# Attention block in exact-split fp32: value matmuls issued ahead of the score matmuls, and four engines' lists reordered

## The reference

```python
xn = layernorm(x, g_in)
q = (xn @ Wq).reshape(b, n, H, DH).transpose(0, 2, 1, 3) * scale
k, v = split(xn @ Wkv)                      # one head each, null_kv put in front
sim = einsum('bhid,bjd->bhij', q, k) + bias # null column, causal and padding masks
attn = softmax(sim, axis=-1)
out = einsum('bhij,bjd->bhid', attn, v)     # to b, n, H * DH
return x + layernorm(out @ Wo, g_out)
```

## Time and profile before

| what | value |
|---|---|
| median of three runs | 1016.31 us (1016.21 to 1018.83) |
| the profiled execution | 1017.48 us, span 1015.7 us |
| TensorE busy | 989.0 us (97%) |
| GpSimd busy | 834.8 us (82%) |
| VectorE busy | 767.9 us (76%) |
| ScalarE busy | 658.6 us (65%) |
| mean granted TensorE clock | 0.995 |

### The profile page before, as it was taken

The page is one execution under the profiler, slowest core; times in us unless marked ns, Lnnn a source line. Parts: engine busy times, 40 slices in busy tenths (PEclk is TensorE's granted clock), DMA queues, the critical chain, the costliest instruction groups (busy, mean ns, idle before and its releaser), DMA issues.

```text
span 1015.7 us, 43757 instructions
## 1 busy us (share of the span) xinstructions
PE 989.0 (97%) x14250; PEld 869.1 (86%) x14250; DVE 767.9 (76%) x3553; ACT 658.6 (65%) x2622; POOL 834.8 (82%) x1503
## 2 busy tenths in 40 slices
PE   7889999999999999999999999999999999999987
PEld 5879888888888888888888888888888888888875
DVE  5976787777887777787777887777787777786664
ACT  5846676665676665676665676666676666675563
POOL 4877888888888888888888888888888888888786
PEclk9998999999999999999999999999999999999999
DMA  8422223223232332323323232232323223222112
GB/s 240 118 79 73 86 72 87 82 68 98 64 107 73 80 87 60 105 69 87 79 70 96 68 106 72 76 90 55 109 70 86 78 71 96 68 70 67 37 44 63
DMA packets 93774, 84.04 MB, mean 83 GB/s; under 512 B 25328, under 2 KB 67824, under 8 KB 93552
## 3 DMA queue, kind: packets, MB, share of 16 engines
q1 hardware_dynamic: 92496, 81.05, 29.9%
q10 hardware_dynamic: 1056, 0.04, 0.1%
HBM read 40.12 MB, written 16.78 MB: 56 GB/s over the span
## 4 chain that ended last, share of the span: by engine, by line
PE 89%; POOL 4%; SPq 3%; issue 2%; DVE 1%; DMA 1%; ACT 1%; POOLq 0%; DVEq 0%; ACTq 0%
PE ps_proj L569 39%; PE ps_pv L546 22%; PE ps_pv L553 11%; PE ps_s L507 10%; PE ps_pv L532 8%; SPq L369 1%; POOL bias_b L1222 1%; POOL w_nrm L1231 1%; DMA q_sb<-in_fside_16xSxS_dram 0%; SPq L344 0%; SPq L379 0%; SPq L338 0%; POOL bias_c L1320 0%; POOL y_nrm L1271 0%; POOL y_out L1275 0%
## 5 line engine op out<-in xcount | busy, mean ns | idle before, releaser
L1031 ACT ACTIVATE exp_bot<-logit_bot,neg_max 128x129 f32<-128x129 f32 x512 | 201.4, 398 | 211.0 <-DVE neg_max L693 208.2
L1222 POOL TENSOR_TENSOR bias_b<-bias_c,mask_add 128x256 f32<-128x256 f32 (+1 forms) x512 | 297.9, 612 | 26.8 <-DVE neg_max L693 26.4
L569 PE MATMUL ps_proj<-xt_hi,wq_hi 128*128 128x256 f32 x1024 | 299.0, 292 | 6.0 <-ACT v_raw L1083 3.7
L569 PE MATMUL ps_proj<-xt_hi,wq_lo 128*128 128x256 f32 x1024 | 285.0, 278 | 0.0
L569 PE MATMUL ps_proj<-xt_lo,wq_hi 128*128 128x256 f32 x1024 | 284.6, 278 | 0.0
L693 DVE CUSTOM_DVE_ANT_0 logit_bot<-ps_s,bias_b 128x128 f32<-128x128 f32 x512 | 128.5, 289 | 139.7 <-PE ps_s L507 123.1
L569 PEld LDWEIGHTS ps_proj<-xt_hi,wq_hi 128*128 128x128 f32 x1024 | 193.4, 189 | 21.2 <-issue 10.5
L1231 POOL TENSOR_TENSOR w_nrm<-exp_bot,w_inv 128x256 f32<-128x256 f32 x256 | 157.9, 617 | 63.0 <-DVE w_inv L702 61.6
L546 PE MATMUL ps_pv<-wo_hi,o_hi 128*128 128x512 f32 x488 | 194.1, 398 | 1.5 <-DVE o_lo L715 1.4
L569 PEld LDWEIGHTS ps_proj<-xt_hi,wq_lo 128*128 128x128 f32 x1024 | 194.0, 189 | 0.7 <-issue 0.5
L569 PEld LDWEIGHTS ps_proj<-xt_lo,wq_hi 128*128 128x128 f32 x1024 | 193.6, 189 | 0.0
(11 more groups left out here) (114 smaller groups left out, 1747.3 us busy)
## 6 DMA issues: line engine op xcount, KB each, us to landing
x_in<-in_x_dram SPq DMA_DIRECT2D x32, 512.0 KB, 4.1
x_split<-xn SPq DMA_DIRECT2D x480, 32.0 KB, 1.9
v_rep<-v_raw SPq DMA_DIRECT2D x256, 32.0 KB, 1.9
x_res<-in_x_dram SPq DMA_DIRECT2D x128, 64.0 KB, 1.9
x_res<-in_x_dram SPq DMA_DIRECT2D x64, 128.0 KB, 2.6
out_dram<-y_out SPq DMA_DIRECT2D x128, 64.0 KB, 1.7
out_dram<-y_out SPq DMA_DIRECT2D x64, 128.0 KB, 2.3
w_raw<-in_L_cond_Wq_dram SPq DMA_DIRECT2D x4, 512.0 KB, 7.6
```

What stands on the lines that cost most here:

```text
L569: mm = pe.matmul(ps[:, 0:TOK], w[:, k, cols], xt[:, slot, k], start=(j == 0), stop=(j == len(todo) - 1))
L1031: ins = nc.scalar.activation(out_[:, s, j], in_[:, s, j], ACT.Exp, bias=neg_max[:, s, k:k + 1], scale=-1.0, accum_out=w_sum[:, s, k:k + 1])
L1222: ins = nc.gpsimd.tensor_tensor(out_, bias, key_mask, ALU.add)
```

## The change

Five lists are reordered, and one wait is added; what is computed stays the same. On TensorE, the `values` of a visit come ahead of the `scores` of the same step. On VectorE, the first of the four `heads_lo` of a visit comes ahead of the `logits` of that step, the other three stay where they were. On ScalarE, `heads_hi` comes ahead of both halves of the step's exponentials at every visit; before, at `t` = 6 and 14, the later half of the exponentials came ahead of it. On SyncE, in the first body (`p = 0`) the values of the second group are spread before the mask load and before `split_x(3)`. GpSimd waits for VectorE's three pieces of `wo_lo` before it makes the fourth.

```diff
@@ SyncE, body, p = 0
                     split_x(BY_PE)
                     next_x(0)
+                    spread_v(2 * p + 1)
                     next_mask()
                     split_x(2 * p + 3)
                     next_x(1)
-                    spread_v(2 * p + 1)
@@ TensorE, body
                 for t in steps(first, last):
+                    for batch, back in due("pv", p, t, first, last):
+                        values(p, batch, back)
                     if t % 2 == 0 and t < CP:
                         scores(p, t)
-                    for batch, back in due("pv", p, t, first, last):
-                        values(p, batch, back)
                     for f, slot, kind, i in front_parts(p, t, first, last):
                         front(f, slot, kind, i)
@@ VectorE, body
                         early = parts[:1] if not list(due("heads", p, t, first, last)) else []
+                        for batch, back in due("heads", p, t, first, last):
+                            heads_lo(batch, 0)
                         if t < CP:
                             logits(n, t)
...
                         for batch, back in due("heads", p, t, first, last):
-                            for g in range(4):
+                            for g in range(1, 4):
                                 heads_lo(batch, g)
@@ ScalarE, body
                     n = CP * p + t
-                    if t < CP and t % CG != STEP_HEADS:
-                        exponentials(n, t, 1)
                     for batch, back in due("heads", p, t, first, last):
                         for g in range(4):
                             heads_hi(batch, g)
-                    if t < CP and t % CG == STEP_HEADS:
+                    if t < CP:
                         exponentials(n, t, 1)
-                    if t < CP:
                         exponentials(n, t, 0)
@@ GpSimd, first_group
                 pool.wait_ge(wo_hi_made, WP)
+                pool.wait_ge(wo_lo_made, WP - 1)
                 nc.gpsimd.tensor_tensor(wo_piece(wo_lo, WP - 1), raw_piece(WP - 1, OT // WP),
```

## The result

The changed kernel takes 1036.14 us (median of 4 runs, 1034.39 to 1037.18), the kernel before, beside it, 1017.31 us (1016.21 to 1018.83): a ratio of 1.0183, 95% interval 1.0164 to 1.0202. It is slower by 1.8% where I forecast 1012.6 us, and above the range (to 1018.0). The profiled span grew from 1015.7 to 1032.6 us, by 16.9.

A forecast was written before the change was run, and what follows sets the result against it. TensorE was taken as the bound, busy throughout the steady loop. Terms -6.5 + 9.9 - 5.7 - 1.5 = -3.8 us gave 1013.7 profiled, forecast as 1012.6 us for the timed median; range 1008.0 to 1018.0.

The forecast's parts named there:

- Fetches: Projection matmuls behind the value matmuls at t = 2: breaks without a releaser would be hidden, -1.5 us (0 to -1.9).
- The start: First body: v_rep issued earlier removes TensorE's 3.67 us idle and the slow clock behind it, 6.5 us sooner (5.8 to 7.2).
- The wait of 0.8 without a fall of the clock: Start, before the third projection block: a wait of about 0.8 us is left, with no clock fall expected from it.
- V ahead of S at t = 2 and 10: Value matmuls before score matmuls wait for transposes or y_nrm: 0.34 us at 29 visits, +9.9 us (5.5 to 18.9).
- the restart: Value matmuls at t = 2 and 10 begin 0.14 us after the transposes they waited for, read from one visit.
- the 0.06 for GpSimd: At the value matmuls of t = 2 and 10, y_nrm late by some 0.06 us more in the mean.
- weight load was pulled across the wait: Alternative at the value matmuls' wait: weights loaded early, a visit costs 0.19, the whole some 4 us less; not expected.
- o_lo ahead of the logits at t = 6 and 14: Output matmuls no longer wait for the first o_lo: 0.20 us at 29 visits, 5.7 us won, low bound 2.8.
- GpSimd: not the bound: Rival: GpSimd's later w_nrm delays y_nrm and the value matmuls, 0.65 a visit, sum +5.2, 1021.5 us; chance 0.23.
- the three rivals: GpSimd becomes the bound (1021.5 us, 0.23); value matmuls hardly wait (1008.1, 0.17); the start doesn't pay (1018.0, 0.1).

The follow-up runs named there:

- late o_lo in the old order: Kernel before with SyncE's and GpSimd's edits only, plus the last three o_lo at t = 14 moved behind a copy and two transposes on VectorE: 1028.14 us.
- early o_lo in the new order: Changed kernel with all four o_lo ahead of the logits at t = 6 and 14: 1030.04 us, 1.0153.
- all four written-out kernels: TensorE's loop unrolled in the changed kernel (1016.41 us), the start alone (1010.38), S first at t = 2 (1013.61) and the best kernel (1001.95).
- S first at t = 2: Changed kernel with scores ahead of values again at t = 2 and 10, values still first at t = 6 and 14: 1029.58 us, 1.0148.
- the start alone: Kernel before with only SyncE's and GpSimd's edits, visits still scores then values: 1012.00 us, 0.9974.
- the second profile: The unchanged kernel before, profiled again for its start: 1013.85 us, span 1012.0.
- the best kernel: The start alone with TensorE written out, ScalarE's list as changed, first o_lo between the two steps' logits at t = 6 and 14: 1001.95 us, 0.9870.
- its two looped forms: The best kernel with TensorE's loop kept: 1012.13 us; then also with all four o_lo ahead of the second logits at t = 14 alone: 1007.97 us.
- S first everywhere: Changed kernel with TensorE's order alone undone, scores ahead of values at every visit, loop kept: 1030.38 us, 1.0143.

## Why the prediction was wrong, step by step

**The step that failed is "Fetches", -1.5 us, between 0 and -1.9.** I saw breaks of 0.1 to 0.4 without a releaser in the F behind V, took them for something that a TensorE standing at V would have hidden, and did not ask what they were. They are the array running out of instructions, and with those ahead of S at t = 0, for which my sum had no term, they grew by 17 us. Break (a): O to S went from 5.87 to 6.41; taken over the 5.59, and without the 0.11 of O's slow first matmul in the old figure, 0.17 became 0.82: 13 x 0.65 = 8.5. Break (b): F to O went from 1.59 to 2.27, 13 x 0.68 = 8.9. With +17.4 in place of -1.5 my sum is -6.5 + 9.9 - 5.7 + 17.4 = +15.1; the spans differ by 16.9.

The cause of (a) is shown, from both sides: late o_lo in the old order bring it (+16, of which 2 are the array's own wait), early o_lo in the new order take it away, and without the jump there is none of it, with the last o_lo anywhere from 1.16 to 2.73 after O's start: S then starts 0.32 after the start of O's last matmul in all four written-out kernels, against 1.54 in S first at t = 2 with its loop. By the Trainium skill (Runtime: NRT & Kernel Launch, section "Instruction fetch mechanics") a sequencer fetches the next page of instructions while it executes the current one, in a purely sequential way, and a taken branch to a page outside the window must wait for that page. The runs agree: 16 KB a packet, 9 packets a pair with the jump and 7 without, and breaks of this kind only with the jump. That crossing a page is otherwise "mostly hidden", as that section of the Trainium skill says, holds for the written-out kernels (between 85 and 940 us no break of over 0.15 us that is not a wait for data) and not for (b).

For (b) the runs show less. At its full size it needs V ahead of S at t = 2 and the loop: F to O is 1.52 with S first at t = 2 and 1.49 to 1.50 written out, against 2.27. It is not always gone with S first: the other loops of that order have 1.59 to 1.76. In the kernel before, the fetch next to this visit started 0.29 us before V (mean of 13), in the changed one 1.29 after V's start. How much of that shift comes from V's wait and how much from S now standing behind V was not separated.

**The start: right in size for the execution I read, in part by luck, and too large for others.** The wait of ScalarE for v_rep is gone, the clock's row is at 9 throughout, SyncE issued x_split(3) from 56.90 (I had it start as before, at 56.08; in the start alone it is 58.16), the third F waited 0.82 us (about 0.8 forecast), and V of step 14 is where I put it (77.4):

```profile
74.41 0.38 PE L569 MATMUL ps_proj<-xt_hi,wq_hi 128*128 128x256 f32 x1 [0.82 <-DVE q_sb L777]
...
77.33 1.43 PE L532 MATMUL ps_pv<-wt,v 32*64 32x128 f32 x80
```

But 87.68 belongs to that one execution. Measured against the second profile, 82.98, the changed start's 81.00 is worth 2.0 us, and the start alone gained 2.7 in the timed runs. My sum stood on one profile of a stretch whose cost varies, and 2.0 of the 6.7 us lie ahead of the first O (49.83 to 47.80), where of the start's edits only GpSimd's added wait acts, which I had put at nothing; how much of the 2.0 is its doing was not separated.

The wait of 0.8 without a fall of the clock was luck as well. TensorE's wait for the copy of q1, which hangs on x_split(3), is 0.82 to 2.32 us in the twelve profiles with these edits, and the changed kernel's is the shortest. In four of them (the best kernel, its two looped forms, and S first everywhere; waits of 1.89 to 2.32) the granted clock fell again behind it, to 0.89 in the mean from 70 to 85 us; behind 1.89 and 2.12 us in two others it stayed at 1.00. The best kernel has the longest:

```profile
74.40 0.38 PE L569 MATMUL ps_proj<-xt_hi,wq_hi 128*128 128x256 f32 x1 [2.32 <-DVE q_sb L780]
```

```profile
75.50:82.50 7.00, 7.00 (x141) 6.54 (x141) 3.37 (x19) 4.77 (x15) 5.54 (x11) 0.76 0.18 49
```

**V ahead of S at t = 2 and 10: right, the total better than its terms.** 0.37 to 0.40 us a visit against 0.34, put down to the transposes in 29 waits. y_nrm ended some 0.01 us before them in most of these, so the profile does not tell the two apart, and taking away one wait alone would have won next to nothing. V started 0.20 behind the transposes in the visit shown (530.39 to 530.59), 0.25 in the mean; I had 0.14 from one visit. So the restart was there and longer than I had it, while the 0.06 for GpSimd is not seen. No weight load was pulled across the wait: V's first began at 530.55, 0.16 behind the transposes' end.

**o_lo ahead of the logits at t = 6 and 14: right, and half the truth.** O's second matmul is 0.23 behind the first (518.73 to 518.96) where it was 0.34; 5.0 of the 5.7 us were won, counted block by block. I looked only at o_lo(0), the one that TensorE's array waits for, and let the other three go behind two steps' logits since O doesn't need them so soon. The sequencer does.

**GpSimd: not the bound in the changed kernel.** It still idled before the y scale, 19.3 us in 39 waits where it was 31.5 in 34, so 0.5 of cushion instead of 0.93. In the changed kernel written out the cushion is nearly gone (4.6 us in 6 waits) and V waits for y_nrm.

```profile
POOL small L1252 <- DVE y_mv L729: 19.3, 39, 1.4
```

None of the three rivals was what happened in the changed kernel; all reckoned with waits for data only.

## What to carry to other kernels

A gap in the profile whose releaser is "issue", at the same place of every round, may be a fetch of instructions, and may be a wait that the profile does not name (the 2.7 us at V above): look where the instruction queue's packets lie, and at the last wait ahead of them, and write the loop out to tell. On an engine whose loop jumps, a semaphore must come early enough for the sequencer and not only for the array; here one that came 1.5 us later cost 16 us in 14 rounds, and matmuls' waits for its data were 2 of them. Writing the bounding engine's loop out removes this (some 18 us in the changed kernel, 10 in the best), but not where the next wait for data takes up the gain (1.6 of 4 us left in the old order). And one profile of a start-up stretch is not its cost: profile it twice before pricing a change to it.

## What the runs showed of the hardware that I had not expected

- TensorE's instructions come in 16 KB packets of 0.9 to 2.3 us, 1.0 to 1.1 in the median. A loop round that needs 7 packets in straight code took 9 with the jump.
- Behind the jump, the fetch started 1.2 to 1.5 us after the last late semaphore, took 1.0 to 1.2, and the first matmul started 1.9 us after its end: 4.3 to 4.4 us from the semaphore to the block behind the jump. Coming earlier than 1.24 us into the O won little, since no fetch started before 2.7.
- Two profiles of one kernel differed by 4.7 us at the same block 85 us in, 2.5 us of it ahead of the first O, 0.7 in the length of one wait, and the rest about a stretch at the lower clock that was shorter in one of them.
- Two subtractions of the same size, on VectorE and GpSimd at once, did not both run at their own pace in the two profiles that show it: the one that started later took 3.46 us on VectorE (1.22 to 1.34 in its place elsewhere) and 3.38 on GpSimd (2.40 to 2.42 when alone).
